# Delta rule of a four-stage kernel: unrolled, and cut into two phases for each pair of heads

## The reference

```
q, k, v, z = x @ W_qkvz                      # 128 columns of each per head
q, k, v    = silu(causal_conv(q, k, v, 4 taps))
q = l2norm(q) / sqrt(128);  k = l2norm(k)
beta = sigmoid(b);  g = cumsum over the chunk of -exp(A_log) * softplus(a + dt_bias)
tri = tril(beta * (k @ k.T) * decay, -1)     # 64 x 64 for each chunk
Tm  = inverse(eye + tri)
v_new = Tm @ (v * beta);  k_cum = Tm @ (k * beta * exp(g))
for each chunk of 64 rows, in order:         # 8 chunks in a sequence
    v_n = v_new - k_cum @ S
    out = (q * exp(g)) @ S + tril(q @ k.T * decay) @ v_n
    S   = S * exp(g_last) + (k * exp(g_last - g)).T @ v_n
h = rmsnorm(out) * silu(z);  y = h @ W_out over all 8 heads
```

## Time and profile before

| | us |
|---|---|
| time, median of 3 runs (range) | 3685.12 (3682.16 to 3687.61) |
| the profiled execution's own time | 3688.41 |
| its span | 3686.7 |
| in the span: TensorE busy | 3110.8 (84%) |
| VectorE busy | 2405.8 (65%) |
| ScalarE busy | 1354.5 (37%) |
| GpSimd busy | 1024.4 (28%) |
| DMA queue for data, share of 16 engines | 7.5% |

### The profile page before, as it was taken

The page is one execution under the profiler, slowest core; times in us unless marked ns, Lnnn a source line. Parts: engine busy times, 40 slices in busy tenths (PEclk is TensorE's granted clock), DMA queues, the critical chain, the costliest instruction groups (busy, mean ns, idle before and its releaser), DMA issues. The chain is left out here.

```text
span 3686.7 us, 86810 instructions
## 1 busy us (share of the span) xinstructions
PE 3110.8 (84%) x32443; PEld 2201.8 (60%) x32443; DVE 2405.8 (65%) x5179; ACT 1354.5 (37%) x4204; POOL 1024.4 (28%) x1623
## 2 busy tenths in 40 slices
PE   7999996599778888888888888888888888888598
PEld 3444442366556666666666666666666666666465
DVE  4666664788636766676665765775676666766466
ACT  2344332233333433343343433443343334333254
POOL 3455544178511122112211211221122111211011
PEclk8999997799869999999999999999999999998799
DMA  2111111000010001000100000010000100000000
GB/s 77 32 33 33 30 34 36 7 1 1 13 27 22 14 16 30 14 15 16 29 15 16 21 22 16 15 29 16 15 14 16 30 14 15 29 18 2 24 18 29
DMA packets 93930, 78.90 MB, mean 21 GB/s; under 512 B 54992, under 2 KB 68320, under 8 KB 93664
## 3 DMA queue, kind: packets, MB, share of 16 engines
q1 hardware_dynamic: 93664, 75.18, 7.5%
HBM read 57.70 MB, written 4.85 MB: 17 GB/s over the span
## 5 line engine op out<-in xcount | busy, mean ns | idle before, releaser
L1394 DVE SCALAR_TENSOR_TENSOR gd_Y<-gd_bk,gd_cwh,gd_Y 128x511 f32<-128x511 f32 (+2 forms) x576 | 403.6, 743 | 77.8 <-ACT gd_Y L1287 75.4
L1562 PE MATMUL gd_bk<-gd_xT,gd_wh 128*128 128x512 f32 x768 | 417.7, 648 | 1.2 <-DMA gd_wh<-in_L_attn_W_qkvz 1.2
L1464 DVE COPY_PREDICATED gd_U<-gd_mU,gd_bk 128x256 f32<-128x256 int32 x320 | 142.7, 446 | 253.5 <-PE gd_bk L1646 177.5
L390 DVE TENSOR_REDUCE at_nm<-at_ring 128x2 f32<-128x256 f32 (+3 forms) x256 | 199.3, 821 | 148.0 <-PE at_ring L531 148.0
L1486 DVE SCALAR_TENSOR_TENSOR gd_V<-gd_bk,gd_cneg,gd_VV 64x128 f32<-64x128 f32 x512 | 161.3, 348 | 187.2 <-PE gd_bk L1675 186.2
L1630 PE MATMUL gd_bk<-gd_L,gd_NT 64*64 64x64 f32 x5120 | 208.4, 226 | 85.1 <-DVE gd_L L1466 78.2
L1356 ACT COPY gd_O<-gd_bk 64x128 f32<-64x128 f32 x512 | 125.6, 260 | 397.8 <-PE gd_bk L1675 397.0
L1630 PEld LDWEIGHTS gd_bk<-gd_L,gd_NT 64*64 64x64 f32 x5120 | 180.1, 139 | 134.1 <-issue 131.9
L1336 ACT COPY gd_ZS<-gd_bk 128x256 f32<-128x256 f32 x320 | 118.5, 373 | 381.6 <-PE gd_bk L1630 375.4
L1641 PE MATMUL gd_bk<-gd_U,gd_ZS 64*64 64x64 f32 x5120 | 229.7, 229 | 23.7 <-ACT gd_ZS L1336 12.4
L1680 PE MATMUL gd_bk<-gd_V,gd_KK 64*128 64x128 f32 x1024 | 203.9, 316 | 48.0 <-DVE gd_V L1486 46.8
(11 more groups left out here) (352 smaller groups left out, 6871.7 us busy)
## 6 DMA issues: line engine op xcount, KB each, us to landing
gd_wh<-in_L_attn_W_qkvz SPq DMA_DIRECT2D x64, 512.0 KB, 4.5
gd_gb<-gates SPq DMA_DIRECT2D x128, 64.0 KB, 4.1
X<-in_L_attn_x SPq DMA_DIRECT2D x8, 512.0 KB, 8.6
at_QT<-at_QS SPq DMA_DIRECT2D x128, 32.0 KB, 2.0
at_KT<-at_KS SPq DMA_DIRECT2D x128, 32.0 KB, 2.0
at_OC<-at_Ob SPq DMA_DIRECT2D x128, 32.0 KB, 1.9
at_RC<-inverse SPq DMA_DIRECT2D x128, 32.0 KB, 1.8
out_x<-X SPq DMA_DIRECT2D x8, 512.0 KB, 2.9
```

Source lines behind the costliest of these rows:

```text
L390: nc.vector.tensor_reduce(nm[v % 2][:, k, c0:c0 + HS + 1:HS], set_of(s, 2 + p)[:, :, 0:n], AX.X, ALU.max).then_inc(max_done, 1)
L1394: ins = nc.vector.scalar_tensor_tensor(out, bk[e][j][:, 0:W - s], cwh[e][:, CV[j], CONVK - 1 - s:CONVK - s], out, ALU.mult, ALU.add)
L1562: ins = nc.tensor.matmul(bk[e][(0, 1, 2, 2)[j]][:, :], wh[e][:, k, WCOL[j] * DK:(WCOL[j] + 1) * DK], xT[:, k, :], start=k == 0, stop=k == ...
```

## The change

All loops of stage C are unrolled in Python: every pair has its own instructions, and counts and addresses are constants. The three parts become two phases. `q` is the pair whose recurrence runs and `f` = `q` + 1 the next one.

- **Phase 1**, nine slots `n` = 0 to 8: head 0 of `q` is at chunk `n`, head 1 at chunk `n` - 1. Chunk 0 needs no product with the state, which is zero: its update uses `VV`, and the state is a copy. In between stand, for pair `f`, the key and gate projections (slots 0, 1), the six key taps (slots 1 to 3, two in each), the decays (slot 2), silu and square of the keys (slots 3, 4), key norms, transposes and Gram matrices (slots 3 to 5), the scaled keys (slots 5, 6), the value projection (slots 6, 7), and the lower matrix with level 0 (slots 7, 8).
- **Phase 2**, the five levels of `f`: with value taps (levels 1, 2), query projection (before and in level 1), query taps (levels 3, 4), values and queries through silu, query norms, and the outputs of `q`: scaled in level 2, transposed in level 3, and the output projection of a sequence in levels 4 and 5, two of its four tiles in each.
- Silu is one ScalarE instruction, of its own function, in place of a tanh and a VectorE multiply. Sums of squares are a square 128x512 on ScalarE of the tile that is not transposed, then four products 128x1 with a column of ones on TensorE for each head, and a copy. Queries are no longer transposed.
- Buffers that pair `f` fills while `q` is read are doubled (`PQ`, `KK`, `AT`, `zz`, `gb`, `cneg`). The small tables are read in place, so GpSimd's copies of them go, and `xs` goes with ScalarE's copy into it.

The core of the diff (helpers first, ScalarE's order of work, then VectorE's, then TensorE's):

```diff
-            nc.scalar.activation(TH[e][:, :], Y[e][j][:, :], ACT.Tanh).then_inc(th_done[e], 1)
-                last = nc.scalar.activation(TH[e][:, t * P:(t + 1) * P], bk[e][j][:, t * P:(t + 1) * P], ACT.Square,
-                                            accum_out=(ssk, ssq)[j][:, e, t:t + 1])
...
-            if nxt:
-                project(it + 1, n // 4, n % 4 // 2, n % 2)
...
+    def gate_out(f, e):
+        act.wait_ge(zp_mm[e], f + 1)
+        ge(act, h_done[e], f - 1)
+        nc.scalar.activation(flat(zz[e][f % 2][:, :, :]), F1[e][:, :], ACT.Silu).then_inc(z_silu[e], 1)
...
+    def keys_out(f, e):
+        act.wait_ge(k_conv[e], f + 1)
+        ge(act, gq_mm[e], f)
+        ge(act, kt_mm[e], f)
+        nc.scalar.activation(kT[e][:, :], YK[e][:, :], ACT.Silu).then_inc(k_silu[e], 1)
+        act.wait_ge(k_silu[e], f + 1)
+        ge(act, nq_mm[e], f)
+        nc.scalar.activation(SQ[e][:, :], kT[e][:, :], ACT.Square).then_inc(k_sq[e], 1)
...
+    def front(f, n):
+        if n in (0, 1):
+            keys_first(f, n)
+        if n in (1, 2):
+            gate_out(f, n - 1)
+        if n == 2:
+            decays(f, 0)
+            decays(f, 1)
+        if n in (3, 4):
+            keys_out(f, n - 3)
+        if n in (4, 5):
+            key_norms(f, n - 4)
+        if n in (7, 8):
+            values_first(f, n - 7)
...
+    def front_early(f, n):
+        if n in (1, 2, 3):
+            for i in range(n * 2 - 2, n * 2 - 1):
+                keys_tap(f, i // 3, i % 3 + 1)
+        if n == 8:
+            lower(f, 1)
+    def front_late(f, n):
+        if n in (1, 2, 3):
+            i = n * 2 - 1
+            keys_tap(f, i // 3, i % 3 + 1)
+        if n in (5, 6):
+            keys_scaled(f, n - 5)
+        if n == 7:
+            lower(f, 0)
+        if n == 8:
+            first_level(f, 0)
+            first_level(f, 1)
...
+    def keys_scaled(f, e):
+        dve.wait_ge(kt_mm[e], f + 1)
+        nc.vector.tensor_tensor(KK[e][f % 2][:, :, :], tiles(F0[e]), spread(KF_, f, e), ALU.mult)
+        ge(dve, kc_mm[e], f)
+        nc.vector.tensor_tensor(KE[e][:, :, :], tiles(F0[e]), spread(EG_, f, e), ALU.mult).then_inc(kk_done[e], 1)
...
+    def level(f, e, l):
+        dve.wait_ge(y_mm[e], f * (LEVELS - 1) + l)
+        last = nc.vector.copy_predicated(U[e][:, :, :], wide(mU[l]), chunks(A_[e], 1))
+        if l < LEVELS - 1:
+            last = nc.vector.copy_predicated(L[e][:, :, :], wide(mL[l]), chunks(A_[e], 0))
+        last.then_inc(u_done[e], 1)
...
+        for l in range(1, LEVELS):
+            if l == 1 and has(f):
+                for s in range(1, CONVK):
+                    values_tap(f, 0, s)
+            if l == 2 and has(f):
+                for s in range(1, CONVK):
+                    values_tap(f, 1, s)
+            if l == 3 and has(f):
+                for s in range(1, CONVK):
+                    queries_tap(f, 0, s)
+            if l == 4 and has(f):
+                for s in range(1, CONVK):
+                    queries_tap(f, 1, s)
+            if l == 5 and has(f):
+                values_scaled(f, 0)
+                values_scaled(f, 1)
+            for e in E2:
+                if has(f):
+                    level(f, e, l)
+                if l == 2 and has(q):
+                    heads_scaled(q, e)
...
+    def keys_in(f, e):
+        pe.wait_ge(w_in[e], 16 * (f + 1))
+        pe.wait_ge(xt_act, seq(f) + 1)
+        pe.wait_ge(xt_dve, seq(f) + 1)
+        ge(pe, vnc_done[e], f)
+        project(F0[e], f, e, 1, kp_mm[e])
+    def gate_in(f, e):
+        ge(pe, kc_done[e], f)
+        for t in range(TPS):
+            for k in range(DC):
+                last = nc.tensor.matmul(F1[e][:, t * P:(t + 1) * P], xT[:, k, t * P:(t + 1) * P], wh[e][:, k, 3 * DK:4 * DK],
+                                        start=k == 0, stop=k == DC - 1)
+        last.then_inc(zp_mm[e], 1)
+    def queries_in(f, e):
+        pe.wait_ge(u_done[e], f * LEVELS + 1)
+        project(F1[e], f, e, 0, qp_mm[e])
+    def values_in(f, e):
+        pe.wait_ge(kk_done[e], f + 1)
+        project(F0[e], f, e, 2, vp_mm[e])
+    def key_norms(f, e):
+        pe.wait_ge(k_sq[e], f + 1)
+        pe.wait_ge(z_silu[e], f + 1)
+        for t in range(TPS):
+            last = nc.tensor.matmul(F1[e][:, t:t + 1], SQ[e][:, t * P:(t + 1) * P], ones[:, 0:1], start=True, stop=True)
+        last.then_inc(nk_mm[e], 1)
...
+    def front_early(f, n):
+        if n in (0, 1):
+            keys_in(f, n)
+        if n in (4, 5):
+            keys_across(f, n - 4)
+        if n == 7:
+            values_in(f, 1)
+        if n == 8:
+            lower_across(f, 0)
+    def front_late(f, n):
+        if n in (0, 1):
+            gate_in(f, n)
+        if n in (3, 4):
+            key_norms(f, n - 3)
+        if n in (4, 5):
+            key_gram(f, n - 4)
+        if n == 6:
+            values_in(f, 0)
+        if n == 8:
+            lower_across(f, 1)
...
+    for q in range(-1, PAIRS):
+        f = q + 1
+        for n in range(NCH + 1):
+            for e in E2:
+                m = n - e
+                if has(q) and 1 <= m < NCH:
+                    pe.wait_ge(s_done[e], q * NCH + m)
+                    nc.tensor.matmul(A_[e][:, 0:DK], PQ[e][q % 2][:, m // CPT, m % CPT, :, :].rearrange("p s n -> p (s n)"), S[e][:, :],
+                                     start=True, stop=True).then_inc(p1_mm[e], 1)
+            if has(f):
+                front_early(f, n)
+            for e in E2:
+                m = n - e
+                if has(q) and 0 <= m < NCH:
+                    c, t = m % CPT, m // CPT
+                    if m == 0:
+                        pe.wait_ge(vnc_done[e], q + 1)
+                        pe.wait_ge(kc_done[e], q + 1)
+                        moving = VV[e][rows(c), t, :]
+                    else:
+                        pe.wait_ge(w_done[e], q * RS + m)
+                        pe.wait_ge(o1_done[e], q * RS + m)
+                        moving = V2[e][rows(c), t, :]
+                    nc.tensor.matmul(A_[e][:, DK:2 * DK], KK[e][q % 2][rows(c), t, :], moving, start=True, stop=True).then_inc(ds_mm[e], 1)
+            if has(f):
+                front_late(f, n)
+            for e in E2:
+                m = n - e
+                if has(q) and 0 <= m < NCH and m % CPT == CPT - 1:
+                    t = m // CPT
+                    if t == 0:
+                        pe.wait_ge(at_done[e], q + 1)
+                        if ends_seq(q - 1):
+                            pe.wait_ge(y_done, (seq(q - 1) + 1) * TPS)
+                    else:
+                        pe.wait_ge(o_done[e], q * TPS + t)
+                    for c in range(CPT):
+                        source = VV if t == 0 and c == 0 else V2
+                        last = nc.tensor.matmul(B_[e][rows(c), 0:DK], AT[e][q % 2][rows(c), t, :], source[e][rows(c), t, :],
+                                                start=True, stop=True)
+                    last.then_inc(oi_mm[e], 1)
...
+        if has(f):
+            queries_in(f, 0)
+        for l in range(1, LEVELS):
+            for e in E2:
+                if has(f):
+                    pe.wait_ge(u_done[e], f * LEVELS + l)
+                    if l == 1:
+                        ge(pe, s_done[e], f * NCH)
+                    for t in range(TPS):
+                        for c in range(CPT):
+                            last = nc.tensor.matmul(A_[e][rows(c), t * CK:(t + 1) * CK], NTm[e][rows(c), t, :], L[e][rows(c), t, :],
+                                                    start=True, stop=True)
+                    last.then_inc(z_mm[e], 1)
+            if l == 1 and has(f):
+                queries_in(f, 1)
+            if l == 3 and has(q):
+                heads_across(q, 0)
+                heads_across(q, 1)
+            if l == 4 and has(f):
+                values_across(f, 0)
+            if l == 5 and has(f):
+                query_norms(f, 0)
+                query_norms(f, 1)
+            if l >= 4 and ends_seq(q):
+                project_out(seq(q), 2 * l - 8)
+            for e in E2:
+                if has(f):
+                    pe.wait_ge(zs_done[e], f * (LEVELS - 1) + l)
...
+            if l == 4 and has(f):
+                values_across(f, 1)
+            if l >= 4 and ends_seq(q):
+                project_out(seq(q), 2 * l - 7)
+        if ends_seq(f) and has(f + 1):
+            for e in E2:
+                ge(pe, ht_out[e], q + 1)
+            x_in(seq(f) + 1, 0)
+            x_in(seq(f) + 1, 1)
```

More of the change, by code:

```diff
@@ new lines, in delta_rule, with ge, has, seq @@
+        PAIRS = B * HP
+        RS = NCH - 1
+        Wq4 = W_qkvz.rearrange("(c p) n -> p c n", p=P)
+        gates4 = gates.rearrange("(b t h) n -> b h t n", b=B, h=H)
+        def ge(eng, s, n):
+            if n > 0:
+                eng.wait_ge(s, n)
+        def has(q):
+            return 0 <= q < PAIRS
+        def seq(q):
+            return q // HP
+        def head(q, e):
```

(70 more changed lines are left out.)

839 lines of the change are left out of this document (350 added, 489 removed).

## The result

The changed kernel takes **3939.6 us** (median of 4 runs, 3937.1 to 3941.0) beside 3683.6 of the kernel before on the same chip: ratio 1.069 (95% interval 1.067 to 1.071), slower. 3846 was forecast, so the direction and two thirds of the size (162 of 256 us) were there, and 94 us were missing.

What follows compares the result with a forecast made beforehand. Stage C, 2370 of 3686.7 us, was the part changed, with TensorE and VectorE taking turns in its front. 31 pairs x (73.7 - 66.9) = +211 and 8 ends x (16.5 - 22.8) = -50 gave 3846 us; range 3590 to 3960.

Steps and rivals of the forecast that it cites:

- walk: Slot-by-slot sum for one ordinary pair in stage C, engines in list order: 70.3 us at full clock.
- phase 2: The five levels: VectorE bounds levels 2 to 4, TensorE level 5 and the rest; 30.3 us a pair.
- the term for the clock: Two more half-clock stretches of TensorE after waits in phase 1: 3.4 us a pair, bounds 0 and 8.
- half clock for the whole of slots 3 to 7: Rival: TensorE stays at half clock there, +8 us, pair 78.3, time 3988 us; chance 0.12.
- The norms: New one-column products on TensorE: 0.9 us a head, bounds 0.25 to 1.8, three of four on the path.
- two table loads a pair: ScalarE switches between silu and exp in slot 3, each load 1.28 us on the path; 62 to 64 in all.
- slot 3 the longest step: Sign: a step of about 7 us in mid phase 1, TensorE idle behind ScalarE's squares; slot 3 put at 7.3.
- the ends: Extra time where a sequence ends, mainly output projection in levels 4 and 5: 16.5 us against 22.8 before.
- the stall at the loop's turn: VectorE stall of 3.29 us at sequence ends, ended only by "issue"; straight-line code should remove it.
- the rival built on it (3931): Rival: each ScalarE table switch also drains about 1.38 us, 2.66 in all, adding some 85 us; chance 0.03.
- the fillers hide: Rival: front work fits the recurrence's waits, pair 65 us gives 3576, 60 gives 3420; chance 0.22.
- The first pass and the last: Stage C's pass without a recurrence and the one without a front, taken as they were: no change.

Runs made afterwards that it cites:

- e3: Changed kernel plus seven filler matmuls a pair on TensorE in slot 3, results unread: 3887.8 us, ratio 1.054.
- e6: Changed kernel with decay exponentials moved from slot 2 to slot 6, plus eight filler matmuls a pair in slots 3 and 8: 3773.6 us, ratio 1.025.
- e8: Changed kernel with decay exponentials in slot 6, inner product ahead of the late front work, and eight filler matmuls a pair: 3577.2 us, ratio 0.971.
- e7: Changed kernel with each product for key and query norms done twice: 4208.8 us, ratio 1.143.
- e1: Changed kernel with every silu of stage C replaced by tanh, so no table loads and a wrong output: 3855.9 us, ratio 1.045.
- e4: Kernel before with only its loop over pairs unrolled, except on the DMA queue's engine: 3659.2 us, ratio 0.992.
- e10: Changed kernel with only the inner product of each slot put ahead of TensorE's late front work: 3768.7 us, ratio 1.021.
- e5: Changed kernel with decay exponentials in slot 6 and the inner product ahead of TensorE's late front work: 3657.3 us, ratio 0.990.

## Why the prediction was right in direction and 94 us short

Its walk can be laid beside the second pair of the windows above. The column for the clock is an estimate: what each slow group took beyond the same group at full clock (0.95 to 1.05 for norms, 0.71 for state products, and so on).

| | forecast, full clock | measured | of it lower clock | rest |
|---|---|---|---|---|
| slots 0, 1 | 8.7 | 9.0 | 0 | 9.0 |
| slot 2 | 2.8 | 2.9 | 0 | 2.9 |
| slot 3 | 7.3 | 8.4 | 1.2 | 7.2 |
| slot 4 | 4.6 | 6.6 | 2.6 | 4.0 |
| slot 5 | 2.6 | 3.4 | 0.9 | 2.5 |
| slot 6 | 4.9 | 5.0 | 0 | 5.0 |
| slot 7 | 5.0 | 4.8 | 0 | 4.8 |
| slot 8 | 4.1 | 5.0 | 0.5 | 4.5 |
| phase 2 | 30.3 | 32.1 | 1.8 | 30.3 |
| clock | 3.4 | | 7.0 | |
| pair | 73.7 | 77.2 | 7.0 | 70.2 |

**The step that failed is the term for the clock:** "two more such stretches and half of their 6.8 us as lost: 3.4" stands against 7.0. The forecast of the pair without it was 70.3; measured, 70.2, with misses of 0.6 or less in the parts that cancel out. The mechanism was named (waits of TensorE in slot 3, then the lower clock), and so was the price: a stretch at half the clock loses half of itself if TensorE is busy in it. What was too small is the time at the lower level. By the windows it is about 20 us in this pair (5.2 in slot 3, 6.6 in slot 4, 1.8 in slot 5, 2.7 in slot 8, 3.9 in phase 2), where 6.8 was taken, and 17 and 24 in the pairs before and behind it. Of the 20 us some 7 are lost, less than half, since TensorE also waits in them. The rival "half clock for the whole of slots 3 to 7" had 78.3 for a pair and 3988: nearer in size, though wrong in place, since slots 6 and 7 were at full clock in this pair and the query projection was hit. In the pair before it, the value projection of slot 6 was hit and the query projection was not; which stretch falls differs from pair to pair. e3, e6 and e8 show that the clock costs time and can be bought back by work.

**The norms**, 0.9 a head, are near what they take at full clock (0.95 to 1.05 in e8); both key groups of this pair took 1.87, a little above the upper bound of 1.8, and the query groups 1.95 for both heads. What the lower clock adds to them is in the 7.0. That they are on the path is shown by e7.

**Right by rows:** two table loads a pair, 1.28 each, on the path (e1: 84 less for 65); slot 3 the longest step, TensorE idle behind ScalarE's squares; phase 2; the ends, some 18 with the x against 16.5; the stall at the loop's turn gone (e4). By the rule of the Trainium skill, "ScalarE: Activation LUTs", section "What ACT_TABLE_LOAD costs", each switch should have a drain of about 1.38 us beside the load. The timeline shows exponentials 0.02 us after one load's end and silu 0.01 after the other's, with the square's end right ahead of the load, and e1 returns 84 us where the loads alone are 83: the trace does not agree, and the rival built on it (3931) came near the measured time by accident. (The prediction's 85 for it belongs to 62 switches; 64 would give 88.)

**What the walk held and did not see:** that the position of the inner product is a choice. I put it behind the norms, as the list has it, counted its wait in slot 3 rightly, and took it as given. It costs 171 us (e10), more than the tables (84) or the exponentials (107). Alone it does not turn the change into a gain (e10 is 1.021); with the exponentials moved, too, it makes it even with the unrolled kernel before (e5 3657.3, e4 3659.2). The argument for the rival "the fillers hide" was that TensorE's own work is some 51 us a pair. That is too low: in the first pair of e8, at a mean clock of 0.97, TensorE is busy 62.0 us; less 3.7 for the eight fillers (the four at the end of slot 8 take 1.84) and 2 for the clock, about 56 remain (an estimate). So the rival's 60 us for a pair was out of reach, and even e8 does not have its 65. That e8 took 3577 where this rival had 3576 is chance, all the more as e8 is another kernel than the change.

**Sum:** the span grew by 248.6 us. The first pass and the last were rightly taken as unchanged: from the first product with values (L1657, now L1826) to the last it is 1121.9 to 3380.2 before and 1122.1 to 3628.7 after, which is 248.3 more. What was off is the base. The sequence of the earlier trace rows takes 290.4 us, but six of the kernel before, from one transpose of outputs (L1698, 1448.56) to another (3206.77), take 293.0 each on average. Six of the changed kernel (L1693, 1508.33 to 3457.33) take 324.8. So the 94 missing us are about 31 times the 3.6 of the clock, 112, less some 20 for a base that was too short (an estimate).

## What to carry to other kernels

When independent work is woven into a serial chain on engines that work in order, what counts is less how much is put in than what stands behind it: the product that another engine waits for goes ahead of the filler, and a function that needs another table goes where no copy of the chain is behind it. Before forecasting such a change, ask of each engine's list in each step which instruction the chain needs next, and whether it could stand earlier. And cost every thin stretch of TensorE, not only the one behind the longest wait, at both levels of the clock: here 17 to 24 us of a pair of 77 were at the lower one.
